# Waits for keys in every fourth step alone; queries a step ahead; the first logits product in front of the weight sums; the last addition in the next step

## The reference

```
q, k, v = x @ Wq + bq, x @ Wk + bk, x @ Wv + bv      # 16 keys, 16 heads
logits  = q . k * 8 ** -0.5
gates   = sigmoid(logits); pos = reversed cumulative sum of gates
logits += interpolation of (q @ pos_emb) between floor(pos) and ceil(pos)
out     = softmax(logits) @ v @ Wo + bo
```

## Time and profile before

| | us |
|---|---|
| median of three runs | 2865.48 (2863.73 to 2867.63) |
| profiled execution | 2860.1 |
| span of its instructions | 2858.4 |
| TensorE busy | 2352.3 (82%) |
| VectorE busy | 1702.4 (60%) |
| ScalarE busy | 1169.0 (41%) |
| Pool busy | 777.0 (27%) |

### The profile page before, as it was taken

One profiled execution on the slowest core, in us unless ns is written; L12 is line 12 of the kernel. 1 busy time (PEld: TensorE's weight loads), 2 busy tenths in 40 slices (PEclk: granted clock), 3 DMA queues, 4 the chain that ended last, 5 costly groups with the idle time before them and its releaser, 6 DMA issues. The chain is left out here.

```text
span 2858.4 us, 41081 instructions
## 1 busy us (share of the span) xinstructions
PE 2352.3 (82%) x14101; PEld 1418.2 (50%) x14101; DVE 1702.4 (60%) x3205; ACT 1169.0 (41%) x2549; POOL 777.0 (27%) x1431
## 2 busy tenths in 40 slices
PE   3788899999999999998979798898888986455554
PEld 1233345454555544455656565666566754233333
DVE  3455555555555555411268666876677768788883
ACT  0244455555555555543424333443434343222222
POOL 3223333433334434322212222132213121110000
PEclk9788799999999999988989898989889997666666
DMA  5322322222232223000000000000000000000000
GB/s 138 72 60 50 68 65 56 65 52 69 46 76 46 61 61 76 2 16 30 30 30 16 19 4 34 33 17 19 5 34 1 34 5 4 0 4 4 4 4 8
DMA packets 87826, 101.41 MB, mean 35 GB/s; under 512 B 11065, under 2 KB 82369, under 8 KB 83521
## 3 DMA queue, kind: packets, MB, share of 16 engines
q1 hardware_dynamic: 80770, 94.42, 13.5%
q10 hardware_dynamic: 6848, 4.36, 0.6%
HBM read 68.35 MB, written 29.62 MB: 34 GB/s over the span
## 5 line engine op out<-in xcount | busy, mean ns | idle before, releaser
L774 DVE TENSOR_REDUCE maxima<-scores 128x2 f32<-128x1024 f32 (+3 forms) x512 | 421.9, 824 | 538.2 <-PE scores L645 533.1
L493 PEld LDWEIGHTS experts_bank<-w,hidden 128*128 128x128 f32 x4096 | 536.0, 197 | 153.6 <-issue 150.2
L493 PE MATMUL experts_bank<-w,hidden 128*128 128x128 f32 x4096 | 562.6, 282 | 0.0
L882 ACT ACTIVATE probs<-turned 128x512 f32<-128x512 f32 (+3 forms) x1024 | 393.2, 435 | 151.9 <-issue 98.4
L970 POOL TENSOR_SCALAR_AFFINE_SELECT probs<-probs 128x256 f32<-128x256 f32 x512 | 212.4, 415 | 657.0 <-ACT probs L882 656.7
L481 ACT ACTIVATE hidden<-rest_bank 128x512 f32<-128x512 f32 x308 | 183.2, 595 | 454.1 <-issue 270.4
L475 PE MATMUL rest_bank<-xe,w 128*128 128x512 f32 x616 | 346.3, 651 | 24.5 <-POOL xe L464 19.4
L1691 POOL TENSOR_SCALAR shift<-mv2b 128x4 f32<-128x4 f32 x48 | 39.4, 820 | 967.6 <-DVE mv2b L1427 967.6
L1438 DVE TENSOR_TENSOR prod<-q,kv 128x2048 f32<-128x2048 f32 x64 | 146.1, 2284 | 158.5 <-ACT kv L1595 156.9
L481 ACT ACTIVATE hidden<-hidden_bank 128x512 f32<-128x512 f32 x204 | 121.6, 596 | 288.3 <-issue 229.8
L663 PE MATMUL turned<-q_stack,k_stack 51*128 51x512 bf16 (+3 forms) x1024 | 196.0, 319 | 27.7 <-ACT probs L882 16.3
(11 more groups left out here) (237 smaller groups left out, 3324.5 us busy)
## 6 DMA issues: line engine op xcount, KB each, us to landing
mask_all<-mask_scratch SPq DMA_DIRECT2D x32, 1024.0 KB, 5.1
stack_q<-parts_q SPq DMA_DIRECT2D x96, 128.0 KB, 2.5
stack_k<-parts_k SPq DMA_DIRECT2D x96, 128.0 KB, 2.4
q_stack<-stack_q SPq DMA_DIRECT2D x32, 384.0 KB, 5.8
k_stack<-stack_k SPq DMA_DIRECT2D x32, 384.0 KB, 9.4
x<-in_L_attn_batch_dram SPq DMA_DIRECT2D x16, 256.0 KB, 5.4
w<-in_L_ffn_W_dram ACTq DMA_DIRECT2D x16, 256.0 KB, 3.0
out_dram<-x SPq DMA_DIRECT2D x16, 256.0 KB, 2.3
```

The costliest lines, as they stand in the source:

```text
L493: mm = pe.matmul(bank[:, n * P:(n + 1) * P], m.hidden[:, q % 4, n * P:(n + 1) * P], t.w2[:, k, :], start=False, stop=(k == E * F - 1), ski ...
L774: dve.tensor_reduce(mx[:, w % 2, :, p, qt], s_bank[:, :, 0:(qt + 1) * P], AX.X, ALU.max)\
L882: act.activation(probs[:, 2 * p + e, KEYS_AT[kt]:KEYS_AT[kt] + width], st_bank[:, e, 0:width], ACT.Exp, scale=SCALE).then_inc(s_exp, 1)
```

## The change

`Step` learns which step makes which queries, and whether its sum is the one that its keys need. That is so in step 0 alone of the steps that have both.

- The key statistics come first, ahead of the sum, unless the sum is for them; they wait for their own sum only by number. On Pool the keys' root and the sum's root trade the slots k=2 and k=5, and ScalarE scales the sum at k=8.
- The wait for the high half of keys stands only where i is a multiple of 4 (steps 0, 4, 8, 12), and names the last group of the four.
- The queries of group i+1 are made at k=19 of step i, in `w_bank`, and copied at k=20 (for group 0 in the last leading step). The weight sums use the same bank and wait for that copy.
- In steps that attend and finish and where i is not a multiple of 4 ("early"), logits 0 is VectorE's first instruction of the step.
- The last addition of a group comes in the next step, between values 0 and values 1; in step 16 that of the last group stays at the end.

```diff
+def group_of(keys):
+    return ROWS_FIRST + ORDER.index(divmod(keys, R))
 class Step:
...
+        self.queries = 0 if keys == 2 else attend + 1 if attend is not None and attend < GROUPS - 1 else None
+    def sum_is_for_keys(self):
+        return self.summed is not None and self.keys is not None and self.keys % R > 0 and group_of(self.keys) == self.summed
...
         def before_m2(i):
-            return 0 if i == 0 else 4 * i - 3
+            return 3 * i - 4
...
         def pe_queries(pe, i):
-            pe.wait_ge(s_m2_read, before_m2(i) + 1)
+            if i > 1:
+                pe.wait_ge(s_wsum_read, i - 1)
             for j in range(G):
-                mm = pe.matmul(m2[:, j * P:(j + 1) * P], kept[:, i % R, j * P:(j + 1) * P], t.w_at[:, 0:D], start=True, stop=True)
-            mm.then_inc(s_m2, 1)
+                mm = pe.matmul(w_bank[:, j * P:(j + 1) * P], kept[:, i % R, j * P:(j + 1) * P], t.w_at[:, 0:D], start=True, stop=True)
+            mm.then_inc(s_q, 1)
...
         def pe_weight_sums(pe, i):
             pe.wait_ge(s_p, i)
+            pe.wait_ge(s_q_read, min(i + 1, GROUPS))
...
             for k in range(E * F + 2):
+                if k == 19 and step.queries is not None:
+                    pe_queries(pe, step.queries)
                 if step.attend is not None:
-                    if k == 3:
-                        pe_queries(pe, i)
...
         def v_weight_sums(dve, own, i):
             dve.wait_ge(s_wsum, i)
-            own(dve.reciprocal(wsum[:, :], w_bank[:, 0:G * H]))
-            dve.wait_ge(s_vec_q, own.value())
+            dve.reciprocal(wsum[:, :], w_bank[:, 0:G * H]).then_inc(s_wsum_read, 1)
+            dve.wait_ge(s_wsum_read, i)
...
         def v_step(dve, step):
...
-            if step.summed is not None:
+            sum_first, early = step.sum_is_for_keys(), attend and finish and i % R > 0
+            if early:
+                v_logits(dve, own_m, i, 0)
+            if sum_first:
                 m.v_sum_stats(dve, step.summed)
-            elif keys is not None:
+                m.v_sum_add(dve, step.summed)
+            if keys is not None:
+                if keys % R > 0:
+                    dve.wait_ge(m.s_x1, group_of(keys) + 1)
                 v_keys_stats(dve, keys)
+            if step.summed is not None and not sum_first:
+                m.v_sum_stats(dve, step.summed)
             if finish:
                 v_weight_sums(dve, own_q, i)
-            if finish:
                 v_values(dve, own_q, i, 0)
-            if finish:
+                if i > 1:
+                    v_last_add(dve, i - 1, before_m2(i - 1))
                 v_values(dve, own_q, i, 1)
-            if step.summed is not None:
-                m.v_sum_add(dve, step.summed)
-                dve.wait_ge(m.s_x1, step.summed + 1)
-            if step.summed is not None and keys is not None:
-                v_keys_stats(dve, keys)
             if step.gates is not None:
                 m.v_row_stats(dve, step.gates)
             if finish:
                 v_values(dve, own_q, i, 2)
-            if keys is not None:
-                dve.wait_ge(s_m1_read, fill_of["high", keys] + 1)
+            if step.summed is not None and not sum_first:
+                m.v_sum_add(dve, step.summed)
+            if attend and i % R == 0:
+                dve.wait_ge(s_m1_read, fill_of["high", i + R - 1] + 1)
             if finish:
                 dve.wait_ge(s_vsum, 4 * (i - 1) + 3)
-            if attend:
+            if attend and not early:
                 v_logits(dve, own_m, i, 0)
             if finish:
                 v_values(dve, own_q, i, 3)
...
                 v_stats2(dve, own_q, i, 3, lambda j: m2[:, j * P:(j + 1) * P])
-                v_last_add(dve, i, n2)
+                if not attend:
+                    v_last_add(dve, i, n2)
...
         def a_step(act, step, before):
-                if k == 5 and step.summed is not None:
+                if k == (5 if step.sum_is_for_keys() else 8) and step.summed is not None:
                     m.a_sum_scale(act, step.summed)
-                if k == 4 and attend:
-                    a_queries(act, i)
+                if k == 20 and step.queries is not None:
+                    a_queries(act, step.queries)
...
         def p_step(pool, step, before):
-                if k == 2 and step.summed is not None:
+                if k == (2 if step.sum_is_for_keys() else 5) and step.summed is not None:
                     m.p_sum_root(pool, step.summed)
-                if k == 5 and keys is not None:
+                if k == (5 if step.sum_is_for_keys() else 2) and keys is not None:
...
```

More of the change, by code:

```diff
@@ L1234, in experts_and_mixing @@
     s_vprod, s_vsum = sem("weighted_values"), sem("weighted_values_summed")
-    s_wsum = sem("weights_summed")
+    s_wsum, s_wsum_read = sem("weights_summed"), sem("weight_sums_read")
+    s_q, s_q_read = sem("queries_product"), sem("queries_copied")
     s_mixed, s_x2 = sem("mixture_copied"), sem("x_after_last")
@@ L1374, in pe_step @@
             finish, last = step.finish is not None, step.attend is None
-            n2 = before_m2(i) - (1 if last else 0) if finish else None
+            n2 = before_m2(i) if finish else None
             for k in range(E * F + 2):
+                if k == 19 and step.queries is not None:
+                    pe_queries(pe, step.queries)
                 if step.attend is not None:
-                    if k == 3:
-                        pe_queries(pe, i)
                     if k in (4, 6, 9, 14):
@@ L1435, in v_logits @@
             if j == 0:
-                dve.wait_ge(s_m2_read, before_m2(i) + 2)
+                dve.wait_ge(s_q_read, i + 1)
             keys = keys_of(i)[:, :, 0:D]
@@ L1535, in v_step @@
             attend, finish, keys = step.attend is not None, step.finish is not None, step.keys
-            n2 = before_m2(i) - (0 if attend else 1) if finish else None
-            if step.summed is not None:
+            n2 = before_m2(i) if finish else None
+            sum_first, early = step.sum_is_for_keys(), attend and finish and i % R > 0
+            if early:
+                v_logits(dve, own_m, i, 0)
+            if sum_first:
                 m.v_sum_stats(dve, step.summed)
-            elif keys is not None:
+                m.v_sum_add(dve, step.summed)
+            if keys is not None:
+                if keys % R > 0:
+                    dve.wait_ge(m.s_x1, group_of(keys) + 1)
                 v_keys_stats(dve, keys)
+            if step.summed is not None and not sum_first:
+                m.v_sum_stats(dve, step.summed)
             if finish:
                 v_weight_sums(dve, own_q, i)
-            if finish:
                 v_values(dve, own_q, i, 0)
-            if finish:
+                if i > 1:
+                    v_last_add(dve, i - 1, before_m2(i - 1))
                 v_values(dve, own_q, i, 1)
-            if step.summed is not None:
-                m.v_sum_add(dve, step.summed)
-                dve.wait_ge(m.s_x1, step.summed + 1)
-            if step.summed is not None and keys is not None:
-                v_keys_stats(dve, keys)
             if step.gates is not None:
@@ L1597, in a_queries @@
         def a_queries(act, i):
-            await_(act, passed["scalar"], s_m2, before_m2(i) + 1)
-            act.activation(q[:, :, :], m2[:, :].rearrange("p (g d) -> p g d", g=G), ACT.Copy).then_inc(s_m2_read, 1)
+            await_(act, passed["scalar"], s_q, i + 1)
+            act.activation(q[:, :, :], w_bank[:, :].rearrange("p (g d) -> p g d", g=G), ACT.Copy).then_inc(s_q_read, 1)
         def a_kink_heights(act, i, j):
@@ L1711, in p_step @@
                 if k == 16 and finish:
-                    await_(pool, passed["pool"], s_m2_read, before_m2(i) + 1)
+                    await_(pool, passed["pool"], s_m2_read, before_m2(i) + 2)
                     norm2(1)
                 if k == 20 and finish:
-                    await_(pool, passed["pool"], s_m2_read, before_m2(i) - (1 if step.attend is None else 0) + 3)
+                    await_(pool, passed["pool"], s_m2_read, before_m2(i) + 3)
                     norm2(2)
```

## The result

The changed kernel takes 2794.54 us (median of three runs, 2789.39 to 2794.99) against 2865.48: 70.9 us less, ratio 0.975, 95% interval 0.9733 to 0.9766. I had forecast 2789 and 76.8 less. The profiled execution took 2789.4 us, its span 2787.7.

What follows compares the result with a forecast made beforehand. VectorE and TensorE were taken to alternate, neither full. Savings of 30, 7.8, 15, 5.5, 9.4, 0.8, 2 and 7.2, less 0.9, made 76.8: median 2865.5 to 2788.7 us, forecast 2789; eight in ten within 2752 to 2835.

Steps and rivals of the forecast that it cites:

- The turning of the keys (steps 2, 3, 6, 7): Expert steps with a sum: values 3 starts 8.1 us earlier; 6.5 saved in 3 and 7, 8.5 in 2 and 6.
- Steps 1, 5, 9: Steps without a sum: 1.65 of TensorE idle time and 0.9 of moved queries saved, 2.6 a step, 7.8 us.
- Step 10: Sixteen items and no gates: the 8.5 of step 2 less 3 for two further items, 5.5 us saved.
- Step 11: No items, but a key and a sum: of 16.2 us of VectorE waits, 9.4 saved.
- Steps 4 and 8: Gap at the turning 4.3, its low-clock stretch 2.3 and queries 0.9 saved: 7.5 us each, 15 together.
- Steps 12 and 16: Step 12 waits about 3.5 for keys in place of 4.25, saving 0.8 us; the last step is unchanged.
- Steps 13 to 15: 2 us saved in all; idle time 4.6 with mixes at full clock or 6.9 at the low one, against 6.3.
- The leading step: Second of three before step 0: TensorE's gap of 4.39 and its low-clock stretch go, 7.2 us; moved queries cost 0.9.
- Two gaps for one: Late relu and mix 0 each stop TensorE with a low-clock stretch in ten expert steps: 2831 us; chance 0.20.
- Uncovered mixes at 1.2 GHz: Eight early expert steps: clock stays low from the gap before mix 0 until mix 2, 2907 us; chance 0.06.
- Keys off the path already: TensorE's order alone sets the step, idle time only changes place: within 5 of 2865 us; chance 0.05.
- TensorE has room: Matmul busy time overstates TensorE's load; all VectorE waits of 156.9 and 64.2 us go: 2644 us; chance 0.04.

Runs made afterwards that it cites:

- the key order alone: The kernel before with only the key statistics ahead of the weight sums, the sum's addition later and matching GpSimd and ScalarE slots: 2813.97 us.
- the late product: The changed kernel with the first logits product behind the third values product in every step, 2789.64 us, or only in steps with expert work, 2780.0 us.
- the run with the rows early: The changed kernel, first logits early only in steps without expert work, GpSimd weighting a new group's first expert rows ahead of the previous step's last root: 2771.89 us.

## Why the prediction was right, and where not

The total came out within 6 us, but in part by luck: the steps below were off by up to 7 us each way, +7.2 and +0.8 against -6.3, -3.0, -2.3, -1.7 and -0.65, and these cancel. The mechanism was right. Of the signs, VectorE's wait for keys fell to 4 times and 26.8, the last addition's to 4.0 and TensorE's at the turning to 3.1, as forecast; step 3 is 8.6 shorter, not 6 to 7.

*The turning of the keys (steps 2, 3, 6, 7).* Right, and the heart of it: the gap and its slow mix go, values 3 waits for mix 2. Forecast 30, measured 37.2. The term with the wrong size is the 2.0 that I added for a low clock at mix 0. I had put 2.3 us of waiting there; it came as 1.74 (the late relu, from Pool's held root) and 0.56, 2.30 in all, and neither brought the clock down. That is 8 over four steps. Values 3 is at S+30.1, not S+32.3.

*Steps 1, 5, 9:* 7.8 forecast, 7.7 measured, but as 2.2, 0.6 and 4.8, not 2.6 each. I took all three to be like step 1. In step 9 mix 3 had run at the low clock (3.32), which is 1.91 now; in step 5 the weight sums grew from 5.58 to 6.89. The sum is right by luck. *Step 10:* 5.5 and 5.4. *Step 11:* 9.4 and 10.2.

*Steps 4 and 8.* 15 forecast, 8.7 measured. The gap at the turning does go, but I took the start of these steps as unchanged. On TensorE in step 4, first in the changed kernel, then in the kernel before:

```profile
1724.67 2.08 PE L475 MATMUL rest_bank<-xe,w 128*128 128x512 f32 x2 [4.47 <-POOL xe L464]
1726.54 6.93 PE L1337 MATMUL rest_bank<-acc,ident 128*128 128x64 f32 x32
...
1736.92 2.07 PE L489 MATMUL experts_bank<-b,mask_t 8*128 8x128 f32 x8
1738.92 2.08 PE L493 MATMUL experts_bank<-w,hidden 128*128 128x128 f32 x8
```

```profile
1763.71 1.53 PE L489 MATMUL experts_bank<-b,mask_t 8*128 8x128 f32 x8
1765.17 1.16 PE L493 MATMUL experts_bank<-w,hidden 128*128 128x128 f32 x8
```

The gap is the old one, but the low clock behind it lasts two products longer: they took 1.53 and 1.16. Why it does stays open. With them the 0.9 of the moved queries is spent. The sum's addition also waits 4.97 here where it waited 1.86, and logits 0 still 4.73 for the high keys. Values 3 of step 4 comes 5.5 earlier (S+44.2 for S+49.7), and the stretch behind it grew by 0.8.

*Steps 12 and 16.* 0.8 and 0 forecast, 2.2 and 1.7 lost. The kernel before, and then the changed one, on TensorE: mix 0 of step 12 and mix 3 of step 16.

```profile
2512.12 1.94 PE L1337 MATMUL rest_bank<-ident,hidden 128*128 128x128 f32 x16 [0.81 <-DVE hidden L1504]
...
2814.19 1.97 PE L1337 MATMUL rest_bank<-ident,hidden 128*128 128x128 f32 x16 [2.46 <-DVE hidden L1504]
```

```profile
2437.26 3.65 PE L1348 MATMUL rest_bank<-ident,hidden 128*128 128x128 f32 x16 [2.51 <-DVE hidden L1515]
...
2741.83 3.62 PE L1348 MATMUL rest_bank<-ident,hidden 128*128 128x128 f32 x16 [2.46 <-DVE hidden L1515]
```

In step 12 the queries had filled TensorE's time ahead of mix 0; with them gone, the gap grew from 0.81 to 2.51 and mix 0 took 1.7 longer. It looks as if the queries had kept the clock up. The run of the key order alone speaks against so simple a reading: there the queries stand at their old place and the gap is 0.81 too, and mix 0 of step 12 still ran slowly:

```profile
2458.81 3.65 PE L1344 MATMUL rest_bank<-ident,hidden 128*128 128x128 f32 x16 [0.81 <-DVE hidden L1511]
```

That step took 77.7 us, and 75.9 before the change. In all three traces the weight sums of step 12 run at the low clock (7.09), behind a wait of TensorE of over 9 us; what differs is whether the clock is back for mix 0. With the queries in place it is back in all of steps 12 to 15 of the kernel before (1.94) and in two of the four with the key order alone; with the queries moved it is back in none of them in the changed kernel (3.65). I had counted the moved queries as a gain of 0.9 a step, and here they gave none; that moving them alone cost the clock is not shown.

In step 16 the gap is the same before and after, the granted clock is 1.00 in both gaps, and behind the gap it falls to 0.50 in the changed kernel alone; why stays open.

*Steps 13 to 15:* 2 forecast, -0.3 measured, with mix 0 at the low clock in all three, as one of my two cases had it.

*The leading step.* 6.3 forecast, 5.65 in the profiles, and the gap of 4.39 is gone. The size is not shown: in the runs above whose leading steps are the changed kernel's, the subtraction of step 0 ended anywhere from 1461 to 1475.

*The early product and the last addition.* I gave the early product no price of its own in the eight expert steps that have one. My own forecast had a hole for VectorE from about S+21 to S+32 there, which would have held its 4.6; the profiles with the late product are 12.2 and 15.8 shorter in steps 3 to 10. I moved the last addition "at no cost"; its new place is what makes the early product bearable.

*The rivals.* "Two gaps for one" had the two gaps but no low clock behind them. "Uncovered mixes at 1.2 GHz" failed as its counter-argument said: all four mixes of step 3 run at full clock (1.94 and three of 1.91). "Keys off the path already" is the opposite of what the run with the key statistics behind the sum shows. "TensorE has room" failed too: the waits were not free time.

## What to carry to other kernels

The longest wait in a profile names the last to arrive, not what would be gained without it: ask which engine's list it hangs on, and put the wait back into the fast version (here it cost 0 us) before you call it the gain. In an engine with an in-order list, work that feeds an early entry must not be pushed back even when the receiving engine seems to have slack; two moves that are each harmless can fill the same room. And look at each gap of TensorE twice, for itself and for what runs slowly behind it; but do not count the slow stretch as certain, since one and the same gap (2.46 us in step 16) had a mix of 1.97 behind it before the change and of 3.62 after it.

## What I had not expected of the hardware

Pool's sum root in step 4 of the run with the rows early, and beside it VectorE:

```profile
1740.44 1.28 POOL L357 TENSOR_SCALAR rstd_e<-mv_e 128x4 f32<-128x4 f32 x1
1741.91 2.96 POOL L359 TENSOR_TENSOR rstd_e<-rstd_e,minus_half 128x4 f32<-128x4 f32 x1 [0.18 <-POOL rstd_e L357]
1745.04 1.79 POOL L361 TENSOR_TENSOR shift_e<-shift_e,rstd_e 128x4 f32<-128x4 f32 x1 [0.18 <-POOL rstd_e L359]
```

```profile
1740.41 1.23 DVE L1506 TENSOR_TENSOR acc<-acc,wsum 128x1024 f32<-128x1024 f32 x1
...
1743.88 0.68 DVE L1542 TENSOR_TENSOR x<-x,y 128x512 f32<-128x512 f32 x1
1744.49 2.28 DVE L1515 TENSOR_TENSOR prod<-acc,kv 128x2048 f32<-128x2048 f32 x1
```

Each of Pool's three instructions on 128x4 elements ends 0.1 to 0.3 us after one of VectorE's that reads two tensors: 1741.72 after 1741.64, 1744.87 after 1744.56, 1746.83 after 1746.77. The same three take 0.23, 1.04 and 0.20 in the root on the key statistics of that step, so the sum's root takes 6.7 us in place of 2.1. In step 3 of the changed kernel the root on the third statistics had only its first instruction held, by 1.8 us, as a reduction followed the product. The sum's root was slow before the change too: its last three instructions took 1.28, 2.96 and 1.19 in step 3. The Trainium skill (GPSIMD Engine Reference, 1. Specifications) says that Pool contends with VectorE's instructions of two SBUF inputs; these rows agree: the small instruction ends only with one of VectorE's.
